# A fused perceiver layer: TensorE's upper-layer loop turned to begin with the token steps, one score run of eight, and the expert-row loads moved to the end of a turn

## The chip, the cores and the metric

The kernel runs on one core of one Trainium2 chip. The metric is the device time of one execution in microseconds (us); lower is better. TensorE is called PE, VectorE DVE, ScalarE ACT, GpSimd POOL and SyncE SP.

## The reference, cut to what matters

All tensors are float32. 32 sequences of 64 tokens with 512 features go through three residual blocks:

```python
x = x + cross_attention(layernorm(x), ctx)     # ctx: 32 x 1601 x 512, one head of 512
x = x + self_attention(layernorm(x))           # 16 heads of 32, causal, with a bias in the denominator
x = x + ffn(layernorm(x))                      # two mixture layers with a gelu between them

def kmoe(x, W, A, B, scale, bias, ...):        # 64 experts, the 2 best of each token
    vals, idx = top_k(x @ W.T, 2); probs = softmax(vals)
    Y = einsum("nkoi,nij,nkpj->nkop", A[idx], xs, B[idx])
    return einsum("nkop,nk->nop", Y, probs).reshape(...) * scale + bias
```

In the upper mixture layer a normalised row pair of tokens (1024 numbers, a 32 x 32 matrix) is multiplied by its expert's A (64 x 32) from one side and by B (64 x 32) from the other; the lower layer goes back from 64 x 64 to 32 x 32.

## The kernel before, in words

The program is written per engine: each engine runs its own list of instructions in order, and semaphores hold the lists together. No planner sets the order; it stands in the code.

**Cross attention** (lines 560 to 789). The 32 sequences are worked on in 16 pairs p. Of each pair the context stands in two halves (7 and 6 tiles of 128 rows), each in one of five slots of SBUF. DVE transposes the context in blocks (`blocks`, L600 to 609, two transposes for a step), PE multiplies a block with the queries (`score`, L590 to 598, 16 steps for a pair), DVE takes the greatest (`greatest`) and later the denominator (`denominator`, after the blocks of step 6), ACT takes exponentials, and PE multiplies the probabilities with the 13 context tiles (`attend`, L755 to 763). PE's list for pair p is: transposes of the probabilities of p - 1, then the 16 score steps of p with the tiles of p - 1 between them, then the last six tiles (L776 to 784). The transposed blocks lie in a ring of four places; for the pairs 2 to 12 (`WIDE`) it has nine. Each tile that PE has finished raises `s_pv`, and SP's transfer of the context three halves ahead waits for that count: a first part (4 tiles) after the fourth tile, a second after the seventh (L653 to 657). The rest rows of a sequence go as five small transfers (L207).

**Self attention** (to about 834 us) is not touched.

**The mixture layers.** The upper layer goes in four turns T of 512 tokens' rows. PE's list for a turn (L2414 to 2448):

1. `gather_up`, eight times: products with one-hot choices that gather B for each token. POOL stages the tables two ahead (`stage_table`, L1880 to 1883), ACT copies the results out (L2165).
2. `rows` (L1535): transposes of the x3 rows of turn T + 1. They read `x3s`, which SP loads (L1829 to 1835) when DVE has transposed it (`s_xt`), PE has transposed it (`s_xf`) and PE has gathered three times (`s_gu`).
3. For T > 0, `logits_dn` (L2261): the lower layer's router logits of turn T - 1, unrolled, 128 products (256 matmuls and 256 weight loads). Then the upper layer's logits of T + 1 (L1551), `fold_dn` (L2269) and `turn_logits` (L1561).
4. `steps_up` (L2383 to 2387): eight laps of an inner loop with two token steps each: `first_up` (L2298), ACT's copy (L2181), `second_up` (L2317), DVE's bias (L2021), ACT's gelu (L2192, L2186). POOL copies the operands of both products (`stage_a`, L1909, and `stage_b`, L1917).
5. Transposes of the one-hot choices of T + 1 and T - 1 (L1568).

Items 2 and the upper half of 3 are skipped by a condition in turn 3, `logits_dn` in turn 0. The rows of the experts' A come by indirect transfers that POOL issues (`experts_rows`, L1391, four a turn, 1 MB each); DVE transposes each into a factor (`factor_a`, L1402), and `stage_a` can start when all four are done. POOL's loads 0 and 1 of turn T + 1 stand in steps 7 and 8 of turn T, load 2 behind the last step, and load 3 in turn T + 1 when two factors are done. SP's list for turn T is: load x3 for T + 1, store the four quarters of the activations h (1 MB each, L1839), and in turn 0 only also store x2 and x3 of the last quad (L851) and wait until they have landed. SP's waits before the x3 load:

```python
                sp.wait_ge(s_xt, 8 * T + 8)
                sp.wait_ge(s_xf, 4 * T + 4)
                sp.wait_ge(s_gu, 8 * T + 3)
```

Of the kernel before, what the change touches and what calls it, by code (L numbers as in the profile page):

```python
# [25 lines left out]
SPARE = {}  # L26
# [532 lines left out]
def cross(nc, block, sem, zone, area, spare, more, temp, ps, a, ident, qbias, halves, slots, qs, s_c, s_qs, s_qd, early):  # L559
# [178 lines left out]
    def _(pe):  # L738
# [33 lines left out]
        for p in range(1, PAIRS):  # L772
# [3 lines left out]
            for g in range(4):  # L776
                transpose_prob(p - 1, g)
            for db in range(STEPS_S):
                if db in (4, 8):
                    for j in ((0, 1, 2, 3) if db == 4 else (4, 5, 6)):  # L780
                        attend(p - 1, j)
                score(pe, p, db)
            for j in range(7, TILES):
# [914 lines left out]
def mixture(nc, block, arena, early, ps, a, first, rest, out):  # L1698
# [105 lines left out]
    def _(sp):  # L1804
# [23 lines left out]

        for T in range(T_N):  # L1829
            if T + 1 < T_N:  # L1830
                sp.wait_ge(s_xt, 8 * T + 8)
                sp.wait_ge(s_xf, 4 * T + 4)
                sp.wait_ge(s_gu, 8 * T + 3)
                for t in range(2):
                    sp.dma_start(x3s[:, t, :], x3_d[2 * T + 2 + t, :, :]).then_inc(s_x3, 16)
            if T + 1 < T_N:
                for q in range(4):
# [33 lines left out]
    def _(pool):  # L1871
# [95 lines left out]
        for T in range(T_N):  # L1967
# [7 lines left out]
            for n in range(STEPS):  # L1975
                stage_b(T, n)
                if n + 2 < STEPS:
                    stage_a(T, n + 2)
                if n == 6 and T + 1 < T_N:
                    exponential("up", T + 1)  # L1980
                if n in (7, 8) and T + 1 < T_N:
                    experts_rows(T + 1, n - 7)
                if n == 10 and T:
                    exponential("dn", T - 1)
            if T + 1 < T_N:
                experts_rows(T + 1, 2)
                stage_table(T + 1, 0)
                stage_table(T + 1, 1)
        for j in range(EARLY):
            stage_unit(j)  # L1990
        stage_unit(EARLY)
# [263 lines left out]
    def _(pe):  # L2255
# [113 lines left out]
        def second_dn(n, u):  # L2369
# [10 lines left out]
                                         start=True, stop=True)  # L2380
            last.then_inc(s_s2, 1)

        def steps_up(T):  # L2383
            with pe.Fori(T * 8, T * 8 + 8) as i:
                first_up(i * 2)
# [25 lines left out]

        pe.wait_ge(early.s_t, 12 * 16)
        pe.wait_ge(s_fold, 2)
        with pe.Fori(0, T_N) as T:  # L2414
            pe.wait_ge(s_ohe["up"][0], T + 1)
            pe.wait_ge(s_bias, T * STEPS + CREDIT)
            apart(pe, SPARE)
            with pe.Fori(T * 2, T * 2 + 2) as j:
                gather_up(j * 4, 0)
                pe.wait_ge(rest.r2, rest.r2_all)  # L2420
                gather_up(j * 4 + 1, 1)
                gather_up(j * 4 + 2, 2)
                for e in range(2):
                    pe.wait_ge(s_ohe["dn"][e], T - 1 + CREDIT)
                gather_up(j * 4 + 3, 3)
            with pe.If(T < T_N - 1):
                for t in range(2):
                    pe.wait_ge(s_geu, T * 8 + 5 + t + CREDIT)
                    rows(pe, T + 1, t, ROW_BANKS[2 * t:2 * t + 2])
            pe.wait_ge(s_geu, T * 8 + 8 + CREDIT)  # L2430
            with pe.If(T > 0):
                pe.wait_ge(s_gelu, T * STEPS)
                pe.wait_ge(s_wr, 32)
                apart(pe, SPARE)
                logits_dn(4)
            with pe.If(T < T_N - 1):
                logits_up_turned(pe, T + 1, 6)
            with pe.If(T > 0):
                fold_dn(T, 7)
            with pe.If(T < T_N - 1):  # L2440
                turn_logits(pe, T + 1, 6)
            steps_up(T)
            with pe.If(T < T_N - 1):
                transpose_choices(pe, "up", 2, T + 2)
            with pe.If(T > 0):
                with pe.If(T < T_N - 1):
                    pe.wait_ge(s_bias, T * STEPS + STEPS + CREDIT)
                    transpose_choices(pe, "dn", 6, T)
        with pe.Fori(0, 2) as p:
            for b in range(4):  # L2450
                unit_first(p, b)
# [54 lines left out]
```

## Time and profile before

| | us |
|---|---|
| three runs | 1232.98, 1235.85, 1237.30 (median 1235.85) |
| the profiled execution | 1234.49 |
| its span in the profile | 1232.7 |
| PE, PE's weight loads | 1165.7, 774.0 busy |
| DVE, ACT, POOL | 790.9, 508.4, 286.0 busy |
| mean granted clock of PE | 0.987 of full |

A row of a timeline has: start in us, duration in us, engine, line, operation, output <- input (partitions x elements), the number of instructions merged, and in brackets how long the engine had been idle before it and what released it ("issue": nothing that the profile shows). Two neighbouring groups of PE overlap a little, since matmuls are pipelined; start to start is the better measure. SPq is SP issuing transfers. Where several issues are merged, the duration covers the waits between them. A row of a table by stretches has: stretch, its length, busy us and instructions of PE, PE's weight loads, DVE, ACT and POOL, the granted clock of PE as a share of full speed (1.00 is the level of 2.4 GHz, 0.50 that of 1.2 GHz), the share of the DMA engines that is busy, and GB/s.

### The profile page before, as it was taken

What the parts mean: (1) busy time and instruction counts of PE and PEld (TensorE: products, weight loads), DVE (VectorE), ACT (ScalarE), POOL (GpSimd) and SP (SyncE); (2) the same over time, 40 slices, a digit from 0 to 9 for tenths busy, and PEclk for the clock granted to TensorE, in tenths of its full rate; (3) what the DMA queues carried; (4) which work ended last, traced back from release to release, by engine and by line L of the source; (5) the groups of instructions that cost most, each with busy time, mean ns of one, the idle gap of its engine ahead of it and who ended that gap; (6) DMA issues with size and microseconds to landing.
All of it is one profiled execution on the core that took longest, in us unless ns stands there. A gap on an engine that the chain in (4) does not pass through costs nothing.

```text
span 1232.7 us, 59579 instructions
## 1 busy us (share of the span) xinstructions
PE 1165.7 (95%) x26847; PEld 774.0 (63%) x26847; DVE 790.9 (64%) x1551; ACT 508.4 (41%) x904; POOL 286.0 (23%) x461
## 2 busy tenths in 40 slices
PE   9999999999999999999999999997888888899995
PEld 6865444434444434666766676675777777789995
DVE  5566777577766774255555555565748686477775
ACT  2323543544344532222212221233647556466763
POOL 1000000000000001022212221223626536246555
PEclk9999999999999999999999999998899999999998
DMA  7886788868887794401110111044627253144423
GB/s 290 277 279 214 254 305 293 291 240 302 298 297 256 268 339 139 105 11 58 68 68 6 62 68 51 35 130 147 237 104 259 109 211 137 48 125 120 120 60 77
DMA packets 65104, 208.33 MB, mean 169 GB/s; under 512 B 11664, under 2 KB 28048, under 8 KB 50864
## 3 DMA queue, kind: packets, MB, share of 16 engines
q1 hardware_dynamic: 62704, 190.24, 45.2%
q0 software_dynamic: 2304, 16.78, 4.0%
q8 instruction: 65, 1.06, 0.3%
q14 instruction: 31, 0.25, 0.1%
HBM read 173.42 MB, written 33.55 MB: 168 GB/s over the span
## 4 chain that ended last, share of the span: by engine, by line
PE 83%; DVE 5%; POOL 3%; issue 3%; DMA 2%; ACT 2%; SPq 1%; DVEq 0%; POOLq 0%; ACTq 0%
PE ps L760 15%; PE ps L596 13%; PE ps L1133 9%; PE ps L2331 5%; PE ps L2365 5%; PE ps L266 5%; PE ps L1247 4%; PE ps L1154 4%; PE ps L508 3%; PE ps L2261 2%; PE ps L2378 2%; PE ps L752 2%; PE ps L2317 2%; DVE arena L2021 2%; PE ps L2298 2%
## 5 line engine op out<-in xcount | busy, mean ns | idle before, releaser
L608 DVE STREAM_TRANSPOSE arena<-arena 128x448 f32<-128x448 f32 (+1 forms) x512 | 257.5, 573 | 27.2 <-PE ps L596 27.1
L760 PE MATMUL ps<-arena 128*64 128x512 f32 x832 | 189.2, 598 | 0.0
L596 PE MATMUL ps<-arena 32*64 32x400 f32 (+1 forms) x4096 | 186.9, 500 | 2.2 <-DVE arena L608 2.0
L596 PEld LDWEIGHTS ps<-arena 32*64 32x64 f32 x4096 | 82.4, 131 | 99.7 <-issue 58.8
L713 ACT COPY arena<-arena 32x2048 f32<-32x2048 f32 x42 | 79.7, 1898 | 138.3 <-DMA arena<-q_n 137.6
L760 PEld LDWEIGHTS ps<-arena 128*64 128x64 f32 x832 | 55.7, 136 | 121.2 <-issue 121.2
L1133 PE MATMUL ps<-arena 128*128 128x256 f32 x512 | 114.2, 381 | 0.8 <-ACT arena L1068 0.8
L934 POOL TENSOR_TENSOR arena<-arena 128x1024 f32<-128x1024 f32 x8 | 19.0, 2369 | 388.1 <-PE ps L760 388.1
L1133 PEld LDWEIGHTS ps<-arena 128*128 128x128 f32 x512 | 96.4, 190 | 17.2 <-issue 3.3
L2181 ACT COPY arena<-ps 128x512 f32<-128x512 f32 x128 | 75.0, 587 | 58.8 <-PE ps L2298 32.4
L2021 DVE SCALAR_TENSOR_TENSOR arena<-ps,arena 128x512 f32<-128x512 f32 x64 | 70.6, 1128 | 36.2 <-PE ps L2317 36.1
L614 DVE TENSOR_REDUCE arena<-ps 128x1 f32<-128x401 f32 (+1 forms) x64 | 32.3, 567 | 82.0 <-PE ps L596 82.0
L2331 PE MATMUL ps<-arena 64*64 64x32 f32 x4096 | 70.3, 218 | 2.7 <-issue 2.7
L2331 PEld LDWEIGHTS ps<-arena 64*64 64x64 f32 x4096 | 68.9, 135 | 3.2 <-issue 2.9
L2031 DVE COPY arena<-ps 128x512 f32<-128x512 f32 x64 | 44.3, 692 | 37.3 <-PE ps L2365 35.2
L1002 DVE SCALAR_TENSOR_TENSOR arena<-ps,arena 128x512 f32<-128x512 f32 x32 | 20.6, 686 | 70.2 <-PE ps L1144 70.2
L631 ACT ACTIVATE arena<-ps,arena 128x384 f32<-128x384 f32 x64 | 36.3, 581 | 70.8 <-DVE arena L622 70.8
L952 POOL TENSOR_TENSOR arena<-arena 128x512 f32<-128x512 f32 x32 | 33.3, 1042 | 138.5 <-DVE arena L1019 138.5
L2365 PE MATMUL ps<-arena 64*64 64x128 f32 x1792 | 61.9, 274 | 0.0
L266 PE MATMUL ps<-arena 128*128 128x512 f32 x128 | 60.2, 605 | 0.0
L1154 PE MATMUL ps<-arena 128*64 128x256 f32 x512 | 58.8, 380 | 0.0
L1247 PE MATMUL ps<-arena 128*128 128x512 f32 x128 | 57.8, 593 | 0.8 <-ACT arena L1109 0.8
(163 smaller groups left out, 1895.7 us busy)
## 6 DMA issues: line engine op xcount, KB each, us to landing
arena<-ctx SPq DMA_DIRECT2D x64, 1024.0 KB
arena<-ctx SPq DMA_DIRECT2D x32, 768.0 KB
h_n<-arena SPq DMA_DIRECT2D x12, 1024.0 KB
arena<-h_n SPq DMA_DIRECT2D x12, 1024.0 KB, 5.1
arena<-x SPq DMA_DIRECT2D x16, 512.0 KB, 4.4
arena<-ctx SPq DMA_DIRECT2D x32, 256.0 KB
x_n<-arena SPq DMA_DIRECT2D x16, 512.0 KB, 3.5
arena<-q_n SPq DMA_DIRECT2D x22, 256.0 KB, 11.0
```

The lines of the kernel that those rows point to most:

```text
L266: x = pe.matmul(ps[:, par, :], early.ats[:, c, par::2], early.xwv[:, c, :], start=c == 0, stop=c == DC - 1)
L596: last = pe.matmul(ps[b * SEQ:(b + 1) * SEQ, tb, 0:WIDTH[tb]], qs[p % 2][r, db, b * SEQ:(b + 1) * SEQ], z[PLACE[at]][r, b, 0:WIDTH[tb]], s ...
L608: vec.transpose(z[PLACE[at]][:, :, g * 224:g * 224 + nt * 32].rearrange("p b (j t) -> p b j t", t=32), slots[slot_of(k)][:, :, 0:nt, db * ...
L713: act.copy(qs[p % 2][tb * 32:(tb + 1) * 32, :, :], qs[p % 2][0:32, :, :]).then_inc(s_copied, 1)
L760: last = pe.matmul(ps[b * SEQ:(b + 1) * SEQ, OB, :], probt[:, j, b * SEQ:(b + 1) * SEQ], slot[:, b, jj, :], start=j == 0, stop=j == TILES - 1)
L1133: last = pe.matmul(ps[:, bank, m % 2 * QROWS:(m % 2 + 1) * QROWS], w[n][:, c, m * P:(m + 1) * P], lnt[:, c, :], start=c == 0, stop=c == DC ...
L1154: last = pe.matmul(ps[e * SEQ:(e + 1) * SEQ, 2 + pair, s2 * 256:(s2 + 1) * 256], lnt[:, c, at:at + SEQ], w["swv"][:, c, :].rearrange("p (m ...
L1247: last = pe.matmul(ps[:, (OUT if more else LAST_OUT) + par, :], aot[:, c, par::2], w["swo"][:, c, :], start=c == 0, stop=c == DC - 1)
L2021: vec.scalar_tensor_tensor(h[:, q, :, at].rearrange("p j g -> p g j"), ps[:, b:b + 2, :].rearrange("p b (g x) -> p (b g) x", x=2 * F1)[:, ...
L2181: act.copy(mid[u].rearrange("p (b x) -> p b x", b=2), ps[:, 2 * u:2 * u + 2, 0:256]).then_inc(s_me, 1)
L2331: last = pe.matmul(ps[k * F1:(k + 1) * F1, 2 * u + t, g * D1:(g + 1) * D1], st_h[u][rows_t, g * F1:(g + 1) * F1], two(st_a[u])[rows_t, k, ...
L2365: last = pe.matmul(ps[q * E:(q + 1) * E, 6 + hf, o * P:(o + 1) * P], slots_dn[slot][r, o, :], oh_st[r, 2 * q:2 * q + 2, :].rearrange("p k ...
```

## The change

Four edits. In cross attention PE's seven tiles of a pair stand in one group between two runs of eight score steps, where they stood as four and three between runs of 4, 4 and 8. SP's x3 load waits for the second gather, and for each half only for the DVE transpose that read that half. POOL's row loads 0, 1 and 2 all stand behind the last step of a turn and behind two table copies. PE's loop over T is turned: gather, rows and logits of turn 0 stand as straight code ahead of it; its body (three laps) begins with the steps and ends with the gather, rows and logits of the next turn; the steps of turn 3 stand behind it. PE executes the same matmuls in the same order.

```diff
@@ -776,8 +776,8 @@
             for g in range(4):
                 transpose_prob(p - 1, g)
             for db in range(STEPS_S):
-                if db in (4, 8):
-                    for j in ((0, 1, 2, 3) if db == 4 else (4, 5, 6)):
+                if db == 8:
+                    for j in range(7):
                         attend(p - 1, j)
                 score(pe, p, db)
             for j in range(7, TILES):
@@ -1828,10 +1828,10 @@
 
         for T in range(T_N):
             if T + 1 < T_N:
-                sp.wait_ge(s_xt, 8 * T + 8)
                 sp.wait_ge(s_xf, 4 * T + 4)
-                sp.wait_ge(s_gu, 8 * T + 3)
+                sp.wait_ge(s_gu, 8 * T + 2)
                 for t in range(2):
+                    sp.wait_ge(s_xt, 8 * T + 4 + 4 * t)
                     sp.dma_start(x3s[:, t, :], x3_d[2 * T + 2 + t, :, :]).then_inc(s_x3, 16)
             if T + 1 < T_N:
                 for q in range(4):
@@ -1978,14 +1978,13 @@
                     stage_a(T, n + 2)
                 if n == 6 and T + 1 < T_N:
                     exponential("up", T + 1)
-                if n in (7, 8) and T + 1 < T_N:
-                    experts_rows(T + 1, n - 7)
                 if n == 10 and T:
                     exponential("dn", T - 1)
             if T + 1 < T_N:
-                experts_rows(T + 1, 2)
                 stage_table(T + 1, 0)
                 stage_table(T + 1, 1)
+                for m in range(3):
+                    experts_rows(T + 1, m)
         for j in range(EARLY):
             stage_unit(j)
         stage_unit(EARLY)
@@ -2380,6 +2379,24 @@
                                          start=True, stop=True)
             last.then_inc(s_s2, 1)
 
+        def gather_tile(T):
+            pe.wait_ge(s_ohe["up"][0], T + 1)
+            pe.wait_ge(s_bias, T * STEPS + CREDIT)
+            apart(pe, SPARE)
+            with pe.Fori(T * 2, T * 2 + 2) as j:
+                gather_up(j * 4, 0)
+                pe.wait_ge(rest.r2, rest.r2_all)
+                gather_up(j * 4 + 1, 1)
+                gather_up(j * 4 + 2, 2)
+                for e in range(2):
+                    pe.wait_ge(s_ohe["dn"][e], T - 1 + CREDIT)
+                gather_up(j * 4 + 3, 3)
+
+        def next_rows(T):
+            for t in range(2):
+                pe.wait_ge(s_geu, T * 8 - 3 + t + CREDIT)
+                rows(pe, T, t, ROW_BANKS[2 * t:2 * t + 2])
+
         def steps_up(T):
             with pe.Fori(T * 8, T * 8 + 8) as i:
                 first_up(i * 2)
@@ -2411,41 +2428,31 @@
 
         pe.wait_ge(early.s_t, 12 * 16)
         pe.wait_ge(s_fold, 2)
-        with pe.Fori(0, T_N) as T:
-            pe.wait_ge(s_ohe["up"][0], T + 1)
-            pe.wait_ge(s_bias, T * STEPS + CREDIT)
+        gather_tile(0)
+        next_rows(1)
+        pe.wait_ge(s_geu, 8 + CREDIT)
+        logits_up_turned(pe, 1, 6)
+        turn_logits(pe, 1, 6)
+        with pe.Fori(0, T_N - 1) as T:
+            steps_up(T)
+            transpose_choices(pe, "up", 2, T + 2)
+            with pe.If(T > 0):
+                pe.wait_ge(s_bias, T * STEPS + STEPS + CREDIT)
+                transpose_choices(pe, "dn", 6, T)
+            gather_tile(T + 1)
+            with pe.If(T < T_N - 2):
+                next_rows(T + 2)
+            pe.wait_ge(s_geu, T * 8 + 16 + CREDIT)
+            pe.wait_ge(s_gelu, T * STEPS + STEPS)
+            pe.wait_ge(s_wr, 32)
             apart(pe, SPARE)
-            with pe.Fori(T * 2, T * 2 + 2) as j:
-                gather_up(j * 4, 0)
-                pe.wait_ge(rest.r2, rest.r2_all)
-                gather_up(j * 4 + 1, 1)
-                gather_up(j * 4 + 2, 2)
-                for e in range(2):
-                    pe.wait_ge(s_ohe["dn"][e], T - 1 + CREDIT)
-                gather_up(j * 4 + 3, 3)
-            with pe.If(T < T_N - 1):
-                for t in range(2):
-                    pe.wait_ge(s_geu, T * 8 + 5 + t + CREDIT)
-                    rows(pe, T + 1, t, ROW_BANKS[2 * t:2 * t + 2])
-            pe.wait_ge(s_geu, T * 8 + 8 + CREDIT)
-            with pe.If(T > 0):
-                pe.wait_ge(s_gelu, T * STEPS)
-                pe.wait_ge(s_wr, 32)
-                apart(pe, SPARE)
-                logits_dn(4)
-            with pe.If(T < T_N - 1):
-                logits_up_turned(pe, T + 1, 6)
-            with pe.If(T > 0):
-                fold_dn(T, 7)
-            with pe.If(T < T_N - 1):
-                turn_logits(pe, T + 1, 6)
-            steps_up(T)
-            with pe.If(T < T_N - 1):
-                transpose_choices(pe, "up", 2, T + 2)
-            with pe.If(T > 0):
-                with pe.If(T < T_N - 1):
-                    pe.wait_ge(s_bias, T * STEPS + STEPS + CREDIT)
-                    transpose_choices(pe, "dn", 6, T)
+            logits_dn(4)
+            with pe.If(T < T_N - 2):
+                logits_up_turned(pe, T + 2, 6)
+            fold_dn(T + 1, 7)
+            with pe.If(T < T_N - 2):
+                turn_logits(pe, T + 2, 6)
+        steps_up(T_N - 1)
         with pe.Fori(0, 2) as p:
             for b in range(4):
                 unit_first(p, b)
```

## Rows read from the trace of the kernel before

**Rows 1.** The page's busy times, all engines.
```profile
PE 1165.7 (95%) x26847; PEld 774.0 (63%) x26847; DVE 790.9 (64%) x1551; ACT 508.4 (41%) x904; POOL 286.0 (23%) x461
```
**Rows 2.** Timeline of PE in one wide pair of cross attention.
```profile
329.93 2.94 PE L596 MATMUL ps<-arena 32*64 32x401 f32 x64
332.80 3.66 PE L760 MATMUL ps<-arena 128*64 128x512 f32 x16
336.39 2.94 PE L596 MATMUL ps<-arena 32*64 32x401 f32 x64
339.26 2.80 PE L760 MATMUL ps<-arena 128*64 128x512 f32 x12
342.00 5.63 PE L596 MATMUL ps<-arena 32*64 32x401 f32 x128
```
**Rows 3.** Timeline of PE in turn 0 of the upper layer, before the steps.
```profile
851.59 0.51 PE L1551 MATMUL ps<-arena 128*64 128x128 f32 x5 [3.91 <-issue]
...
858.77 1.72 PE L2298 MATMUL ps<-arena 32*32 32x64 f32 x128
```
**Rows 4.** Timeline of PE: ends of the steps of turns 1 and 3.
```profile
917.32 1.48 PE L2298 MATMUL ps<-arena 32*32 32x64 f32 x128
...
934.07 0.76 PE L2317 MATMUL ps<-arena 64*64 64x64 f32 x32 [1.55 <-POOL arena L1917]
...
945.18 0.65 PE L1568 MATMUL ps<-arena 128*128 128x128 f32 x4
...
1019.59 1.49 PE L2298 MATMUL ps<-arena 32*32 32x64 f32 x128
...
1044.16 0.69 PE L2317 MATMUL ps<-arena 64*64 64x64 f32 x32 [0.48 <-DVE arena L2021]
```
**Rows 5.** Timelines of SP and PE around the x3 load, turns 1 and 2.
```profile
898.63 0.81 SPq L1835 DMA_DIRECT2D arena<-x_n  x2
...
903.74 3.63 PE L1535 MATMUL ps<-arena 128*128 128x128 f32 x16 [2.94 <-DMA arena<-x_n]
...
957.38 1.96 PE L1535 MATMUL ps<-arena 128*128 128x128 f32 x16 [0.18 <-DMA arena<-x_n]
```
**Rows 6.** Timelines of DVE and PE in pair 13, four places in the ring.
```profile
409.36 0.12 DVE L678 TENSOR_REDUCE arena<-arena 128x1 f32<-128x6 f32 x1
...
417.39 6.09 PE L596 MATMUL ps<-arena 32*64 32x401 f32 x128
```
**Rows 7.** Timelines of DVE and SP in the pair of rows 2.
```profile
325.05 7.01 DVE L608 STREAM_TRANSPOSE arena<-arena 128x448 f32<-128x448 f32 x14
...
345.94 2.04 SPq L207 DMA_DIRECT2D arena<-ctx  x5
...
350.18 7.01 DVE L608 STREAM_TRANSPOSE arena<-arena 128x448 f32<-128x448 f32 x14
```
**Rows 8.** Timeline of POOL: the first factor copies of turns 0 and 3.
```profile
851.75 2.07 POOL L1909 COPY arena<-arena 128x512 f32<-128x512 f32 x2 [7.10 <-DVE arena L1402]
...
1016.96 1.22 POOL L1909 COPY arena<-arena 128x512 f32<-128x512 f32 x2 [6.76 <-DVE arena L1402]
```
**Rows 9.** Table by stretches: clock, DMA share and GB/s in two stretches.
```profile
890.00:893.00 3.00, 2.95 (x117) 2.98 (x125) 3.00 (x3) 0.93 (x1) 0.29 (x1) 0.53 0.99 407
934.00:938.00 4.00, 3.84 (x192) 3.37 (x192) 2.63 (x6) 1.70 (x4) 3.53 (x6) 0.57 1.00 268
```
**Rows 10.** Timeline of PE in the lower layer's first pass.
```profile
1067.75 0.43 PE L2331 MATMUL ps<-arena 64*64 64x32 f32 x16 [1.33 <-issue]
```
**Rows 11.** DMA queues, 934.5 to 938.5 us: packets, MB, share of the engines.
```profile
q0 software_dynamic: 129, 0.96, 94.6%
q1 hardware_dynamic: 2, 0.02, 1.0%
```
**Rows 12.** Instruction queues in 845 to 852 us and, second, in 862 to 1045 us.
```profile
q8 instruction: 2, 0.03, 2.1%
...
q14 instruction: 5, 0.04, 0.1%
```

## The prediction

> **What bounds the kernel now.** Read first the page's busy times: TensorE (PE) is busy 95% of the span [rows 1]; whatever moves the end moves PE's own instructions or the gaps between them. Then read PE's instructions in order of time, for the two places that are edited.
>
> *Cross attention* (to about 490 us). PE never waits. A pair of sequences from p = 2 to 12 ("wide", up to nine blocks ahead) is a fixed string: 4 score steps, 4 context tiles, 4 score steps, 3 tiles, 8 score steps, 6 tiles [rows 2]. Only PE's own pace counts.
>
> *Upper layer* (834 to 1045 us), four turns T. See four kinds of gap. In turn 0, PE stops for 3.91 us before the logits and begins the token steps only at 858.77 [rows 3]. In the steps, VectorE's and POOL's work nearly hides, but in the middle PE waits 1.55 us for POOL's copies [rows 4], because POOL issues two indirect row loads there. Between the steps of turn 0 and of turn 1, PE waits 2.94 us for the x3 rows, which SP could load only after two stores had landed [rows 5]. Between turns 1 and 2 that wait is 0.18 us: on time, with nothing to spare [rows 5].
>
> **The change, part by part.** Against the profiled execution (1234.49 us).
>
> *1. Score runs: one of 8 in place of 4 + 4.* In a wide pair, the stretch from the first score to the third run is 342.00 - 329.93 = 12.07 us. A run of 64 matmuls takes 2.87 (start to start), one of 128 takes 5.56 (its 5.63 less the 0.07 that two groups overlap); 16 context matmuls take 3.59, 12 take 2.74, so 28 take 3.59 + 12 x 0.215 = 6.17. New sum 11.73: 0.34 less, times 11 pairs, 3.7 us gained [rows 2]. VectorE begins a pair's blocks at 325.05, 4.9 us ahead of PE, one step (two transposes) per 1.0 us, so step 8 is there at 333.3 [rows 7] where PE wants it at 334.8: hidden. Pairs 1, 13, 14 and 15 have four places only; there a run of 8 already waits for VectorE and takes 6.09 rather than 5.63. The new first run adds the denominator's two short operations (0.12, and I take the other alike) in VectorE's way: 5.56 + 0.46 + 0.24 + 6.17 = 12.43, 0.36 more, times 4, 1.4 lost [rows 2, 6]. Net **-2.3** (bounds -3.7 and 0). The slot's transfer is released later: its first part after the fourth tile, at 329.93 + 5.56 + 3.59 = 339.1 where it was 336.4, its second after the seventh, at 341.7 where it was 342.0. SP's last issue for it ends at 345.94 + 2.04 = 348.0 now and no later then; the block that reads it starts at 350.18 + 0.5. Hidden, with some 2 us for the last and smallest piece to land [rows 2, 7]; if that cover went, each wide pair would lose what lies beyond.
>
> *2. The loop turned.* The order of PE's instructions stays the same; only what is loop, skip and straight code changes. Before, turn 0 jumped over the unrolled lower-layer logits (512 instructions), and the gap of 3.91 us in which PE waited for nothing visible follows that jump. Now turn 0's part stands straight. PE is free at 847.68 and has about 3 us of logits work; next late is POOL, whose second copy ends at 851.75 + 2.07 = 853.82 [rows 3, 8]. Steps then start at 853.9 rather than 858.77: -4.9. PE will have idled in pieces before, and where it idles the granted clock falls (a stretch at 0.57 lies behind the 1.55 us wait [rows 4, 9]); I charge 0.9 for that. **-4.0** (bounds -5 and 0).
> Price of the turning: the backward jump now lies between one transpose and the steps, where before it lay behind 8 transposes; nothing in the trace shows it bare. Ends: nothing, or a first-pass gap such as the 1.33 us in the lower layer [rows 10] at each of two jumps; I take 0.4, being nearest to the inner loop's jumps, which show nothing. The last turn's steps are a new copy, run for the first time: one such gap, 1.3 (0 to 3.9). **+1.7**.
>
> *3. POOL's row loads 0 and 1 leave steps 7 and 8 for the end of the turn, behind two table copies, with load 2.* The steps of turn 1 take 945.18 - 917.32 = 27.9 us, those of turn 3, which has no such loads, 1044.16 + 0.69 - 1019.59 = 25.3 [rows 4]. Turns 0, 1 and 2 are alike; of the 2.6 some 0.2 is the second pow operation that turn 1 keeps. 3 x 2.4 = **-7.2** (bounds -8.3 and -5.5). Queued behind the moved loads on POOL are only table copies that PE wants once it has gathered from the two that are made ahead: nothing.
>
> *4. What the moved loads collide with.* They now start some 1.5 us before the steps end, three in a row, 3.1 MB, where one (1 MB) was in flight. In that stretch SP also sends the last quarter of h (1 MB) and, after turn 0, x2 and x3 (1 MB), and waits for their landing before it loads the next x3 rows. The trace shows who yields: with two row loads queued the software queue holds 94.6% of the engines for 4 us and the hardware queue 1.0%, while SP is in the midst of its four h stores [rows 11]. Rates: 407 GB/s, and 268 where the two kinds meet [rows 9]; I take 0.36 MB/us. So 2.1 MB more stand ahead: 5.8 us.
> Turn 1: SP gets past the landing of x2 and x3 at 898.63; that comes 5.8 us later, and the load behind it meets a little more traffic: **+6.0** (bounds +3 and +8.5) at PE's wait before 903.74 [rows 5].
> Turn 2: x3 rows land at 957.38 after a load that SP issued only once VectorE had read the old rows; by then the engines had run dry for, as I estimate, 1.6 us, so 5.8 - 1.6 = 4.2. The SP edit (second gather in place of third, each half as soon as its transpose is done) sends half of it 1.1 us earlier, into the same queue: nothing. PE then idles over 4 us and the row transposes take 3.63 as in turn 1 instead of 1.96 [rows 5]: **+5.9** (bounds +1 and +9).
> Turn 3: no x3 load. VectorE's factors come about 1 us later; POOL's two copies, done at 1018.18, have 1.4 us to spare before the steps [rows 4, 8]. **+0.5** (0 to 2).
> Turn 0's x3 load comes one gather earlier; PE did not wait for it: nothing.
>
> By a rule of the Trainium skill, "DMA: Bandwidth & Descriptors", section "Queues, rings and completion order", each DMA engine goes round the queues that have work and changes at packets. The pair of [rows 11] shows one side alone for 4 us, so the trace bears it out at most at whole transfers; by the rule only about one row load would stand ahead, and the time would be that of the second rival.
>
> **Sum.** -2.3 - 4.0 + 1.7 - 7.2 + 6.0 + 5.9 + 0.5 = +0.6 us: 1235.1 against 1234.49. The three runs have a median of 1235.85, 1.4 above; on that scale 1236.5. A measurement of this kernel can tell about 0.3% (3.7 us) from no change.
>
> **The rivals.**
> *A, slower: the turned loop is fetched again on each lap.* Place: the jump from turn 1's and turn 2's logits to the steps. If the target has gone, the gap of [rows 3] comes back, 3.91 us and again about as much with the next block, on two laps: +13, 1249. It decides once the body no longer stays in the engine. For: two instruction packets ran in 845 to 852 us. Against: from 862 to 1045 the queue that brought them (q8) moved none, over three backward jumps [rows 12], and the body is no longer than it was. 0.10.
> The Trainium skill, "Runtime: NRT & Kernel Launch", section "Instruction fetch mechanics", says that a taken branch whose target is outside the two pages at hand forces a fetch before execution goes on. That would price this rival at every lap; the empty queue of [rows 12] speaks against it here.
> *B, faster: the queues alternate.* h, x2 and x3 pass between the row loads; one load, not two, stands ahead, 2.9 us: turn 1 +3.2, turn 2 +1.3 and +1.7 for the slower transposes. Sum -5.0: 1231 on the scale of the median. For: late packets of both queues are mixed in other stretches. Against: [rows 11]. 0.25.
> *C, the turn doesn't do what it says:* the gap before turn 0's steps comes from the first pass itself, not from the skip. Then -4.0 is gone: +4.6, 1240.5. For: 1.33 us gaps in the lower layer's first pass. Against: these are a third of 3.91. 0.12.
> *D, slower: the contention is deeper.* The fourth row load slips ahead of SP's loads too and the queues meet at 268 GB/s: turn 1 +8.5, turn 2 +8.5: +5.7, 1241.5. 0.13.
>
> **How the numbers follow.** My own sum has 0.40. The predicted time is its 1236.5, its own range 1232 to 1241. B reaches down, C and D up; the range 1229 to 1246 leaves out A and the tails of B. Faster by over 0.3% (below 1232.1): most of B and a bit of mine, 0.25. Slower by over 0.3% (above 1239.6): A, D, most of C, a bit of mine, 0.34. Within: 0.41.
>
> **What would show it.** Wide pairs with a period 0.3 us shorter, narrow ones 0.4 longer; turn 0's steps starting where POOL's second factor copy ends; steps of turns 0 to 2 of 25.5 to 26.5 us; PE's waits for x3 of 8 to 9 us in turn 1 and 4 to 5 in turn 2, with SP's landing of x3 late; instruction packets beside turn 3's steps only. Wrong if x3's waits stay below 4 us (B), if the gap stays before turn 0's logits (C), or if q8 is busy in turns 1 and 2 (A).

## The result and the profile after

The changed kernel takes 1238.03 us (median of 20 runs, 1235.81 to 1240.39), the kernel before 1235.69 on the same chip (20 runs). The ratio is 1.0022, interval 1.0012 to 1.0031: 0.22% slower, within the 0.3% that were called no change, and 1.5 us above the predicted 1236.5. The profiled execution took 1238.09 with a span of 1236.3, 3.6 more than before's 1232.7.

A small sum of large terms, then, as forecast. First the page's busy times, which answer to [rows 1]: PE does 3.7 us less in a span that is 3.6 longer, so it waits some 7 us more.

```profile
PE 1162.0 (94%) x26847; PEld 776.4 (63%) x26847; DVE 790.8 (64%) x1551; ACT 508.8 (41%) x904; POOL 283.9 (23%) x461
```

The timeline of PE in a wide pair, as [rows 2], and below it in the narrow pair 13, where [rows 6] stood. The columns are start, us, engine, line, what is computed, count, and in brackets the idle time before with its releaser.

```profile
328.15 5.63 PE L596 MATMUL ps<-arena 32*64 32x401 f32 x128
333.71 6.24 PE L760 MATMUL ps<-arena 128*64 128x512 f32 x28
339.89 5.63 PE L596 MATMUL ps<-arena 32*64 32x401 f32 x128
...
402.52 5.10 PE L596 MATMUL ps<-arena 32*64 32x401 f32 x112
407.93 0.93 PE L596 MATMUL ps<-arena 32*64 32x401 f32 x16 [0.31 <-DVE arena L608]
408.80 6.25 PE L760 MATMUL ps<-arena 128*64 128x512 f32 x28
414.97 6.08 PE L596 MATMUL ps<-arena 32*64 32x401 f32 x128
```

The wide stretch is 339.89 - 328.15 = 11.74 (forecast 11.73), the narrow one 414.97 - 402.52 = 12.45 (forecast 12.43), with a stop for VectorE before the last 16 scores of the run.

The timeline of PE in the upper layer: turn 0 up to its steps (as [rows 3]), the way into turn 1, the way into turn 2, and the start and end of turn 3's steps. Lines behind L1830 carry a number one lower than before (L2297 was L2298).

```profile
846.28 1.97 PE L1551 MATMUL ps<-arena 128*64 128x128 f32 x32 [1.15 <-issue]
...
851.58 1.73 PE L2297 MATMUL ps<-arena 32*32 32x64 f32 x103 [2.58 <-POOL arena L1909]
855.22 0.65 PE L2297 MATMUL ps<-arena 32*32 32x64 f32 x25 [1.91 <-issue]
...
883.26 2.53 PE L2280 MATMUL ps<-arena 64*32 64x128 f32 x144 [1.73 <-ACT arena L1522]
890.46 8.30 PE L2280 MATMUL ps<-arena 64*32 64x128 f32 x368 [4.67 <-issue]
904.77 3.68 PE L1535 MATMUL ps<-arena 128*128 128x128 f32 x16 [6.01 <-DMA arena<-x_n]
...
944.56 0.66 PE L1568 MATMUL ps<-arena 128*128 128x128 f32 x4
960.74 3.67 PE L1535 MATMUL ps<-arena 128*128 128x128 f32 x16 [4.20 <-DMA arena<-x_n]
...
1024.80 2.04 PE L2297 MATMUL ps<-arena 32*32 32x64 f32 x128 [0.36 <-POOL arena L1909]
...
1050.82 2.41 PE L2348 MATMUL ps<-arena 64*64 64x128 f32 x80
```

See three things. The 3.91 us of [rows 3] have become 1.15. A stop of 1.91 us stands inside the first pass of the steps, at their 104th matmul, and one of 4.67 inside the first gather of turn 1, the first execution of that copy. And x3 is late by 6.01 and 4.20 us.

The gap of [rows 3] wasn't alone. A second one stood before the other 27 of the same 32 matmuls (timeline of PE, kernel before), and it is gone as well: 3.91 + 2.59 have become 1.15.

```profile
854.70 3.25 PE L1551 MATMUL ps<-arena 128*64 128x128 f32 x27 [2.59 <-issue]
```

Read as a ledger, with turn by turn the steps and the "front" (from the end of one turn's steps to the start of the next):

| us | before | after | difference |
|---|---|---|---|
| span's start to turn 0's steps | 858.77 | 851.58 | -7.2 (1.8 of it in cross attention) |
| steps of turn 0 | 28.9 | 29.3 | +0.4 |
| front of turn 1 | 29.7 | 38.1 | +8.4 |
| steps of turn 1 | 27.9 | 25.6 | -2.2 |
| front of turn 2 | 24.1 | 31.3 | +7.2 |
| steps of turn 2 | 28.2 | 25.6 | -2.5 |
| front of turn 3 | 22.1 | 23.3 | +1.1 |
| steps of turn 3, and the rest | | | -0.3, -1.4 |

The sum of the differences is +3.6 before rounding. About 1 us of the first row is scatter between traces: run 2 below, which changes nothing ahead of turn 0's steps, starts them at 857.62, 1.15 earlier than the kernel before.

Who is ahead of x3? The timelines of POOL and of SP around the end of turn 0's steps (which is at 880.87). POOL issues three row loads in a row, SP its two stores of x2 and x3, and 14.46 us later, when they have landed, the load.

```profile
879.18 1.08 POOL L1391 DMA_INDIRECT arena<-a_up,arena  x1 [0.16 <-issue]
880.56 0.94 POOL L1391 DMA_INDIRECT arena<-a_up,arena  x1 [0.30 <-issue]
881.80 0.94 POOL L1391 DMA_INDIRECT arena<-a_up,arena  x1 [0.30 <-issue]
...
896.87 0.97 POOL L1391 DMA_INDIRECT arena<-a_up,arena  x1 [0.15 <-issue]
```

```profile
883.46 1.50 SPq L851 DMA_DIRECT2D x_n<-arena  x2
897.92 0.82 SPq L1835 DMA_DIRECT2D arena<-x_n  x2
```

Before, the stores were issued at 890.29 and the load at 898.63 [rows 5], 8.34 later. And the DMA queues (packets, MB, share of the engines), first in 883 to 887 us, where only the software queue moves data though SP's h and x stores are already issued, then in 888 to 892 us, where both do:

```profile
q0 software_dynamic: 163, 1.21, 89.8%
...
q1 hardware_dynamic: 108, 0.88, 52.2%
q0 software_dynamic: 109, 0.76, 47.1%
```

Where nothing stands beside them the same stores start at once: in run 5 they are issued at 856.32, and in 857 to 858 us the hardware queue has 87.2% of the engines.

### The profile page after: what moved, and what is told of

It reads as the page before. It is cut to its first block, busy times and chain, and to the rows that moved or that the text cites. A ratio compares the mean times of both kernels' runs of the same rounds, so it can differ in the third digit from the quotient of the medians.

```text
span 1236.3 us, 59550 instructions
## 1 busy us (share of the span) xinstructions
PE 1162.0 (94%) x26847; PEld 776.4 (63%) x26847; DVE 790.8 (64%) x1551; ACT 508.8 (41%) x904; POOL 283.9 (23%) x461
## 4 chain that ended last, share of the span: by engine, by line
PE 80%; DVE 7%; issue 4%; DMA 3%; POOL 2%; SPq 2%; ACT 1%; DVEq 0%; POOLq 0%; ACTq 0%
PE ps L760 14%; PE ps L596 11%; PE ps L1133 9%; PE ps L2330 5%; PE ps L2364 5%; PE ps L266 5%; PE ps L1247 4%; PE ps L1154 4%; DVE arena L608 3%; PE ps L508 3%; PE ps L2377 2%; PE ps L2316 2%; DVE arena L2020 2%; PE ps L752 2%; PE ps L2260 2%
## 5 line engine op out<-in xcount | busy, mean ns | idle before, releaser
L760 PE MATMUL ps<-arena 128*64 128x512 f32 x832 | 185.8, 596 | 0.0
L266 PE MATMUL ps<-arena 128*128 128x512 f32 x128 | 60.2, 605 | 0.0
```

What stands on the lines that cost most here:

```text
L266: x = pe.matmul(ps[:, par, :], early.ats[:, c, par::2], early.xwv[:, c, :], start=c == 0, stop=c == DC - 1)
L760: last = pe.matmul(ps[b * SEQ:(b + 1) * SEQ, OB, :], probt[:, j, b * SEQ:(b + 1) * SEQ], slot[:, b, jj, :], start=j == 0, stop=j == TILES - 1)
```

## The experiments

Twelve runs in three sets, each set on one chip with runs of the kernel before between them; ratios are to those. "Changed" is the changed kernel.

**1. Score runs alone.** The first hunk of the diff, nothing else:
```
-                if db in (4, 8):
-                    for j in ((0, 1, 2, 3) if db == 4 else (4, 5, 6)):
+                if db == 8:
+                    for j in range(7):
```


> Only the score runs (one of 8 in place of 4 + 4). Theory: wide pairs (2 to 12) 0.34 us shorter each, pairs 1, 13, 14 and 15 0.35 us longer each; in all -1.5 to -2.5 us, and nothing later changes. Rival: the transfer that is released later reaches VectorE's blocks too late and PE waits for them: then the wide pairs save less than 0.2 us each and the whole is 0 to +2 us.

Measured: 1234.37, before 1234.70; ratio 0.9994 (0.998 to 1.0009). Cross attention is 2.0 us shorter (from its first matmul of L752 to the first of L266: 380.28 before, 378.31 here, 378.49 in the changed kernel), and turn 0's steps start 2.1 earlier, at 856.68. Turn 1's start at 917.15, only 0.2 earlier. Timelines of POOL, SP and PE show where the gain went:

```profile
894.79 0.97 POOL L1391 DMA_INDIRECT arena<-a_up,arena  x1 [0.24 <-DVE arena L1402]
...
895.80 0.82 SPq L1835 DMA_DIRECT2D arena<-x_n  x2
...
902.56 3.68 PE L1535 MATMUL ps<-arena 128*128 128x128 f32 x16 [6.11 <-DMA arena<-x_n]
906.16 8.27 PE L2261 MATMUL ps<-arena 64*64 64x128 f32 x256
```

Turn 0's steps end 2.9 us earlier than before (884.76 and 887.64), and the x3 load moves along: 895.80 against 898.63, 2.8 earlier. But here POOL's fourth row load was issued 1.0 us ahead of it, and x3 took 6.76 us to land; before, that load was issued 0.28 behind it, and x3 took 5.11. That is 1.65 of the 2.8. Another 1.0 goes behind the wait, which has grown from 2.94 [rows 5] to 6.11: the 256 matmuls of the lower layer's logits take 8.27 us (granted clock 0.87 in 906.1 to 914.4) where they took 7.27 (1.00 in 907.3 to 914.5). This is one pair of traces; the times alone, with their interval, allow anything from 2.5 us won to 1 us lost.

**2. The row loads alone.** POOL's hunk, on the kernel before; SP's waits stay as they were:
```
-                if n in (7, 8) and T + 1 < T_N:
-                    experts_rows(T + 1, n - 7)
...
-                experts_rows(T + 1, 2)
                 stage_table(T + 1, 0)
                 stage_table(T + 1, 1)
+                for m in range(3):
+                    experts_rows(T + 1, m)
```


> Only POOL's row loads 0 and 1 moved from steps 7 and 8 to the end of the turn. Theory (the moved loads make SP's transfers late): steps of turns 0, 1, 2 shorter by 2 to 3 us each (-7), but PE's wait for the x3 rows rises from 2.94 to about 9 us in turn 1 and from 0.2 to about 5 us in turn 2, row transposes of turn 2 at half clock; in all +4 to +8 us. Rival (x3 is late in the changed kernel because PE's gather of turn 1 ran as first-time code, with a gap of 4.67 us): here that code is resident, the x3 waits stay near 3 and 0 us and the whole is -5 to -7 us.

Measured: 1239.67, ratio 1.0043 (1.0025 to 1.006), +5.3 us by the ratio. Steps of turns 0 to 2: 26.0, 25.6, 25.6, together 7.7 less. Fronts of turns 1 to 3: 37.1, 29.9, 22.9, together 13.9 more; net +6.2 in the trace. The gathers of turn 1 ran without any stop for code, and PE waited all the longer for x3, 11.74 us where about 9 were expected (timeline of PE, turns 1 and 2):

```profile
906.68 3.68 PE L1535 MATMUL ps<-arena 128*128 128x128 f32 x16 [11.74 <-DMA arena<-x_n]
...
962.79 3.45 PE L1535 MATMUL ps<-arena 128*128 128x128 f32 x16 [4.42 <-DMA arena<-x_n]
```

The late x3 is due to the moved loads, and not to the turned loop.

**3. The turn alone.** The two hunks in PE's program only (gather_tile, next_rows and the turned loop).

> Only PE's loop turned. Theory: the gap before the logits of turn 0 goes, steps of turn 0 start right after POOL's second factor copy, 4 to 6 us earlier, run at half clock at first with one gap of about 2 us; the gather of turn 1 has a first-time gap, partly hidden by the wait for x3; 1 us less behind the last step. In all -1 to -4 us. Rival: the first-time code of turn 1's gather and the bare backward jumps (0.5 us each) eat the gain: -1 to +2 us.

Measured: 1228.73, ratio 0.9949 (0.993 to 0.9968), -6.3 us, more than any theory had. (Its profiled execution is the slowest of its seven, and 4.1 us below that of the kernel before.) Timeline of PE before the steps of turn 0 and in turn 1:

```profile
853.45 2.04 PE L2298 MATMUL ps<-arena 32*32 32x64 f32 x128 [2.17 <-POOL arena L1909]
...
892.78 8.13 PE L2281 MATMUL ps<-arena 64*32 64x128 f32 x368 [3.19 <-issue]
901.07 1.96 PE L1535 MATMUL ps<-arena 128*128 128x128 f32 x16 [0.16 <-ACT arena L2165]
```

The steps start 5.3 us earlier. There is no stop inside their first pass here, nor in that of turn 3. The new copy of the gather stops PE for 3.19 us, but in the place of the 2.94 us for which PE waited for x3 before: the front of turn 1 stays 29.7. So the first-pass stop of this copy costs next to nothing. Turn 0's steps end 4.0 us earlier than before (883.67 and 887.64) and turn 1's begin 3.9 earlier (913.38 and 917.32): this gain passes the place of the wait whole. POOL's fourth row load was issued at 899.01 here, 4.0 us behind the x3 load (894.97). And a stop of 1.01 us that stood behind the last step of turn 3 is gone.

**4. Changed, with the row loads back in steps 7 and 8.**

> The changed kernel with POOL's row loads 0 and 1 back in steps 7 and 8. Theory: against the changed kernel the steps of turns 0 to 2 are 2 to 3 us longer each, but PE waits for x3 3 to 4 us in turn 1 and below 1 in turn 2: 6 to 9 us faster than the changed kernel, 3 to 6 us faster than the kernel before. Rival (the moved loads are worth their place): it is slower than the changed kernel.

Measured: 1229.17, ratio 0.9951 (0.9935 to 0.9966), about 9 us below the changed kernel. Fronts 29.6, 24.4 and 22.0, no wait for x3 in turns 1 and 2, where 3 to 4 us and up to 1 were expected. This is the turn with the score runs, and it is as fast as the turn alone: turn 0's steps start 1.9 us earlier than there (851.52) and end at the same time (883.61 and 883.67), since a first-pass stop of 2.11 us stands in them.

**5. Changed, with turn 0's store ahead of the h stores.**
```
+            if T == 0:
+                rest.store_rows(sp)
+                sp.wait_ge(s_out, QUADS * 32)
             (the four h stores)
-            if T == 0:
-                rest.store_rows(sp)
-                sp.wait_ge(s_out, QUADS * 32)
```


> The changed kernel, and turn 0's store of the last activation rows with the wait behind it is moved ahead of the h stores in SP's queue, so that turn 1's x2 and x3 transfers are issued sooner. Theory (x3 is late in turn 1 because its transfer is issued behind the three row loads, which start when turn 0 ends): the 6.0 us wait of the first row matmul of turn 1 shrinks to 0 to 3 us, the 4.2 us wait of turn 2 stays, and the time is 2 to 6 us below the changed kernel's 1238, so 1232 to 1236. Rival (the order in SP's queue is indifferent, since the store itself waits for the row loads on the DMA engines): the wait stays at 5 to 7 us and the time at 1238.

Measured: 1237.56, ratio 0.9981 (0.9971 to 0.9991), by the ratios 5 us below the changed kernel, on another chip. The stores leave at 856.32, before any row load, and x3 is issued 6.2 us behind the end of turn 0's steps (890.20 - 884.04), where the changed kernel needs 17.0; PE no longer waits for it. So much is the order in SP's queue. But the wait of turn 2, which this edit doesn't touch, is gone as well, and so the size of the gain isn't the edit's alone. The timeline of PE at the end of turn 0 shows what else is different:

```profile
878.79 0.60 PE L2316 MATMUL ps<-arena 64*64 64x64 f32 x8
879.77 0.34 PE L2316 MATMUL ps<-arena 64*64 64x64 f32 x5 [0.38 <-issue]
880.48 0.35 PE L2316 MATMUL ps<-arena 64*64 64x64 f32 x6 [0.37 <-issue]
881.21 0.35 PE L2316 MATMUL ps<-arena 64*64 64x64 f32 x6 [0.38 <-issue]
881.94 0.36 PE L2316 MATMUL ps<-arena 64*64 64x64 f32 x5 [0.38 <-issue]
```

PE goes by five or six matmuls and stops for 0.37 us, for nothing that the profile shows, while the row loads run (issued at 878.53, 879.91 and 881.15); the last step's second half takes 5.2 us in place of the changed kernel's 1.5. The same stands in turns 1 and 2. The steps take 30.3, 28.9 and 28.5 us, and the gain of the moved loads is gone; in exchange the loads are issued 5.1 us before the end of turn 1's steps (944.57 - 939.50) and not 1.8 (944.56 - 942.79), so that less of them is left in front of x3.

**6. SP's waits alone.**
```
-                sp.wait_ge(s_xt, 8 * T + 8)
                 sp.wait_ge(s_xf, 4 * T + 4)
-                sp.wait_ge(s_gu, 8 * T + 3)
+                sp.wait_ge(s_gu, 8 * T + 2)
                 for t in range(2):
+                    sp.wait_ge(s_xt, 8 * T + 4 + 4 * t)
```


> The kernel of before, with nothing changed but SP's waits ahead of the x2 transfers (one per half). Theory: nothing, 1234.7 plus or minus 1, and the step spans within 0.3 us. Rival: the earlier start of the first half is worth up to 1 us in each of turns 1 and 2 (1232.5), or it meets the row loads and costs as much.

Measured: 1239.57 against 1239.73, ratio 0.9997 (0.9984 to 1.0011): nothing, as forecast. It served as the trace of before on this chip, and gave one more pair for x3. Timelines of POOL, SP and PE:

```profile
900.42 0.96 POOL L1391 DMA_INDIRECT arena<-a_up,arena  x1 [0.35 <-DVE arena L1402]
...
900.60 0.81 SPq L1835 DMA_DIRECT2D arena<-x_n  x2
...
908.20 3.68 PE L1535 MATMUL ps<-arena 128*128 128x128 f32 x16 [5.31 <-DMA arena<-x_n]
```

POOL's load was 0.18 us ahead, and x3 took 7.60 us.

**7. Changed, with the first of the three loads back in step 7.**
```
+                if n == 7 and T + 1 < T_N:
+                    experts_rows(T + 1, 0)
...
-                for m in range(3):
+                for m in (1, 2):
```


> The changed kernel, with the first of the three row loads issued in step 7 again and the other two left at the end of the turn. Theory (what counts is the bytes that stand in the queue ahead of x3): the x3 wait of turn 1 falls by a third to a half from 6.0 us (3 to 4), that of turn 2 from 4.2 to 1 to 2, the steps of turns 0 to 2 are some 1.2 us longer each (half of what two loads cost); the time is 1234 to 1237. Rival (the queue is held by whatever is in it, one load or three): waits as in the changed kernel, steps longer, 1239 to 1241.

Measured: 1234.57, ratio 0.9969 (0.9953 to 0.9985). There is no wait for x3 in turns 1 and 2 at all; from the x stores to the x3 load it is 883.90 to 893.30, 9.4 us, against 14.5 with three loads and 8.3 with one. "By a third to a half" was wrong: both waits are gone. The two loads were issued 6.5 us ahead of the x stores (883.90 - 877.36), where the three of the changed kernel begin 4.3 ahead (883.46 - 879.18): more of fewer bytes had passed. Part of that lead is the slow last step of this chip (steps 29.9, 28.3, 28.2), so what a load's worth of bytes costs can't be read from this run.

**8. Changed, without moved loads, with the early store, and with runs of eight in wide pairs only.**
```
-                if db == 8:
-                    for j in range(7):
+                if p in WIDE:
+                    if db == 8:
+                        for j in range(7):
+                            attend(p - 1, j)
+                elif db in (4, 8):
+                    for j in ((0, 1, 2, 3) if db == 4 else (4, 5, 6)):
```


> The changed kernel without its moved row loads (they stand in steps 7 and 8 again), with the early store of turn 0, and with the one score run of eight only in the wide pairs 2 to 12, the narrow ones as before. Theory: the turned loop keeps its 5.5 to 6 us, no x3 wait stands in turns 1 and 2, and the narrow pairs no longer give anything back (1.4 us less than with runs of eight everywhere): 1227 to 1229 us. Rival (the score run gives nothing wherever it stands, and the store in front delays turn 0's h): 1229 to 1231.

Measured: 1231.06, ratio 0.9931 (0.9918 to 0.9944) on a chip where before took 1239.73. In microseconds the expectation missed, since it was written for a faster chip; 8.6 us below before is more than it had.

Runs 5 to 8 left a question: the stop and go of run 5 was in every kernel of that set and in none of the first. So the ends of the ladder were run once more, each rung beside its neighbour.

**9 to 12. A ladder on a third chip.** Changed again; with the loads back in steps 7 and 8 (as 4); with the edit of run 8 to the score runs besides; with the early store besides (as 8).

> The changed kernel once more, as the upper end of a ladder of four on one chip. Ratio to the kernel before 1.001 to 1.004. In its trace: the row loads issued 1.5 us after the last step's first matmul, as in the run with the early store. Theory A (the stop-and-go of TensorE in the last step, six matmuls and 0.37 us idle, belongs to kernels in which the loads' transfers meet that step): it is absent here, the steps of turns 0 to 2 are 29, 25.6 and 25.6 us. Theory B (it belongs to the other chip of the second set of runs): the kernel can't tell, and steps of 28 to 29 us may stand here too.

> The changed kernel with its row loads back in steps 7 and 8: the second rung. Ratio to the kernel before 0.994 to 0.997, some 7 to 9 us below the first rung. No x3 wait in turns 1 and 2; steps 28 us, fronts 29.6 and 24.4 us.

> The second rung with the score runs of eight kept only in the wide pairs. Theory (the narrow pairs give back 0.36 us each in four pairs): 0.5 to 1.5 us below the second rung, TensorE's first value matmul (L266) 1.0 to 1.5 us earlier against its first score. Rival: no difference, within 0.5 us.

> The third rung with the early store of turn 0, the same kernel as the earlier run of this combination. Theory (with the row loads in the steps no wait for x3 is left, so the store's place is indifferent): within 1 us of the third rung. Rival (the x3 transfer that lands sooner takes DMA time from the gathers' side): 1 to 2 us either way.

| kernel | median us | ratio to before (1234.23) | interval |
|---|---|---|---|
| 9 changed | 1237.92 | 1.0029 | 1.0015 to 1.0044 |
| 10 row loads back | 1228.10 | 0.9946 | 0.9925 to 0.9967 |
| 11 and runs of eight in wide pairs only | 1227.66 | 0.9946 | 0.9926 to 0.9966 |
| 12 and the early store | 1227.14 | 0.9938 | 0.9918 to 0.9959 |

*9*: the result repeats. The waits for x3 are 6.59 and 4.40, the steps 29.0, 25.6 and 25.6. Its row loads are issued 1.4 to 1.5 us behind the start of the last step's first matmul, as in run 5 (939.50 - 938.04 in turn 1 there), and there is no stop and go. Stops of 0.30 to 0.47 us inside the steps: 13 in run 5, 8 in run 6, 10 in run 7, 8 in run 8, none or one in each of the ten other traces. Run 6 is almost the kernel before, and runs 8 and 12 are the same kernel, with 8 stops there and none here. So theory B holds: they belong to that chip, beside row loads; what they are stays open, and how the changed kernel does there was not run.

*10*: 9.8 us below rung 9. In turn 1 (timeline of PE) the stop for the gather's code stands alone, and x3 is there:

```profile
892.61 7.89 PE L2281 MATMUL ps<-arena 64*32 64x128 f32 x368 [2.91 <-issue]
900.63 1.96 PE L1535 MATMUL ps<-arena 128*128 128x128 f32 x16
```

*11*: cross attention is 1.40 us shorter (377.06 from L752 to L266, against 378.46), the 4 x 0.36 of the prediction; the narrow pair is back to four runs:

```profile
402.08 2.94 PE L596 MATMUL ps<-arena 32*64 32x401 f32 x64
404.95 3.66 PE L760 MATMUL ps<-arena 128*64 128x512 f32 x16
408.55 2.94 PE L596 MATMUL ps<-arena 32*64 32x401 f32 x64
411.42 2.80 PE L760 MATMUL ps<-arena 128*64 128x512 f32 x12
414.15 6.09 PE L596 MATMUL ps<-arena 32*64 32x401 f32 x128
```

But turn 0's steps start only 0.33 us earlier (850.71 and 851.04), and the time doesn't tell the two apart. *12*: within 1 us of rung 11, as expected. PE's program is that of rung 11, but the first-pass stop of 1.91 us that stands in turn 0's steps there is absent here; the steps take 29.4 us for 31.5, and start 0.4 later. Rungs 10 to 12 all beat both kernels; which of the three is best isn't settled.

## Why the prediction was right

The total and its sign against the bound of 0.3% were right; the terms, one by one:

| term | forecast | measured in the changed kernel |
|---|---|---|
| score runs | -2.3 | -1.8 in cross attention |
| turn 0's front | -4.0 | -5.4 at the steps' start (-7.2 less 1.8), +3.3 inside the steps, against run 2 |
| price of turning | +1.7 | 0.4 at each of two jumps; no first-pass stop in turn 3, and 1.0 less behind its steps; the stops are in turns 0 and 1 |
| loads out of the steps | -7.2 | -7.7 in run 2 |
| x3 in turns 1 and 2 | +6.0, +5.9 | fronts +8.4, +7.2; in run 2 +7.4, +5.8 |
| turn 3's front | +0.5 | +1.1 |

**Score runs.** The terms of a pair were right to 0.02 us in wide and narrow pairs, and run 11 shows the four narrow pairs by themselves: 1.40 us. What failed is the step from there to the end: alone they give 0.3 us of 2.0. The prediction had passed every gain ahead of turn 1 on whole: "2.94 <-DMA x_n" [rows 5] as a gap that moves along with the work ahead of it, and the work behind it at its old pace. In run 1 the x3 load did move along, but its transfer became 1.65 us longer behind POOL's fourth row load, and the logits behind the longer wait took 1.0 longer at a lower clock. In the narrow pairs the cover in VectorE's way got thinner: a stop of 0.31 us stands in the middle of the run.

**The turn.** This is the term that was mis-sized: -2.3 with its price, and -6.3 measured alone (4.1 between the two profiled executions). Its parts failed twice. The start of turn 0's steps was right in kind (they begin where POOL's second copy ends, 849.37 + 2.06, and the gap of 3.91 went). The bare backward jump costs 0.4 us each time (0.49 us before the steps of turn 1, 0.47 before those of turn 2, where [rows 4] has next to nothing), 0.8 for both where 0.4 was taken. But the 1.3 us for a first pass in turn 3 never came; the stops sit where PE first runs the gather's second copy and, in some traces, in turn 0's steps. The stop of 3 to 5 us in the gather was not forecast at all, and it is nearly free, because it takes the place of a wait for x3. Of rival C, that the first pass itself was behind the gap, this much is right: 1.15 + 1.91 us of first-pass stops stand in turn 0 where 3.91 + 2.59 stood (the prediction had read the first alone), and the clock is low behind them (the stretch 852 to 860 us at 0.50):

```profile
852.00:860.00 8.00, 6.09 (x322) 5.41 (x307) 3.82 (x6) 2.26 (x5) 4.80 (x8) 0.50 0.01 4
```

The 0.9 us charged for the clock were too few: turn 0's steps take 29.3 rather than 26.0 (run 2, where the loads are out of them too), and only 1.91 of these 3.3 us are the stop. In run 3, which has no stop in them, they take 30.2 where the kernel before took 28.9.

**The row loads.** The mechanism was right as the prediction put it: 5.8 us more ahead of the landing of the x stores, measured 14.46 - 8.34 = 6.1. PE's wait in turn 1 was to be 8 to 9 us; it is 11.74 in run 2, and 6.01 in the changed kernel only because 4.67 us of stop stand ahead of it. On top came what rival D had described: POOL's fourth row load went out ahead of x3's (896.87 and 897.92), and x3 took 6.85 us instead of 5.11. Five traces with it ahead (changed, runs 1, 2, 6 and 9) have 6.76 to 7.60, the one with it just behind has 5.11, and in runs 3, 4 and 10, with it 3.6 to 4.0 us behind, x3 was there when PE came, at most 5.7 to 6.1 us after its issue. No run moved this load alone, so the order is the likely cause and not a shown one. Forecast for the moved loads was +5.2 in all; alone they cost 5.3 by the ratio, on top of the turn 9.8. The difference isn't in x3's transfer. From the end of the steps to the row transposes the moved loads add 7.0 and 4.3 us in turns 1 and 2 of run 2, and 6.6 and 4.1 between run 4 and the changed kernel. It is behind them: from the transposes to the next steps they add 0.4 and 1.5 us in run 2, and 1.9 and 2.9 in the turned kernel. There, in run 4, PE had not waited in turn 1 and the transposes took 1.97 us; in the changed kernel they take 3.68, which the kernel before had paid already (3.63), and turn 2's logits take 8.40 instead of 7.27, at a granted clock of 0.86. Smaller parts are 0.7 us less relief in the steps, 0.6 in turn 3's front and 0.7 in its steps.

So the sum was right by luck, through two errors that met: the turn gives 4 us more, and in its company the loads cost 4 us more.

**The rivals.** A fell: the instruction queue q8 moved 5 packets from 862 to 919 us, where PE first runs the copies of the gather, the transposes and the logits, and 1 from there to 1050. The sign "beside turn 3's steps only" had forgotten that these copies are new too. The page of the Trainium skill that was set against [rows 12], "Runtime: NRT & Kernel Launch", section "Instruction fetch mechanics", would have a fetch at every such jump; in all the turned kernels the stop between the loop's jump and the steps' first matmul stays between 0.47 and 0.57 us, against 1.2 to 4.7 for the stops in code that is run for the first time. B fell in its size, as three loads did hold the stores for over 13 us, but its rule is seen at work from 888 us on, with 52.2% and 47.1%. By the Trainium skill's "DMA: Bandwidth & Descriptors", section "Queues, rings and completion order", the queues take turns at packets all the time; the 89.8% for one of them in 883 to 887, with 2 MB of stores issued on the other, speak against that for the first 4 us. D had the right mechanism; the fronts (+8.4, +7.2) lie at its +8.5 in turn 1 and between forecast and rival in turn 2.

## What to carry to other kernels

A wait in front of an engine isn't a cost that adds up. Ask of everything ahead of it whether the transfer that ends it moves along. A stop of 3 us in the gather, which hardly held x3's transfer, was nearly free. A gain ahead of the transfer's issue is passed on, as the 4 us of run 3 were, unless the transfer meets other traffic by it: in run 1 the load left 2.8 us earlier and the next steps began 0.2 earlier. And where several transfers are moved to a quiet moment, list what the other queues send at that moment and who waits for its landing: 7.7 us of relief inside the steps cost 13.9 us between them. Split a change whose parts meet at one wait, and take the parts that pay: without the moved loads this one is 0.5% faster than the kernel before.

## What was not expected of the hardware

- The first pass of a copy of code stopped PE for 1.3 to 4.7 us in the midst of short matmuls (the 104th of the steps, the 145th of the gather). For the gather it was 4.67 and 3.06 in two traces of the same changed kernel, 2.91 to 4.54 with the row loads back in the steps, and 1.33 in run 7. More DMA traffic beside it doesn't make it longer in any order that these runs show.
- Such a stop can be absent for the same loop: turn 0's steps stopped for 1.9 to 2.5 us in the changed kernel and runs 4, 9, 10 and 11, and not at all in runs 3, 5, 7, 8 and 12. Runs 5, 7 and 9 have the PE program of the changed kernel and run 12 that of run 11, so PE's own code doesn't decide it; what does stays open.
- After three indirect loads (issued from 879.18 to 881.80) the software queue had 89.8% of the engines in 883 to 887 us and the hardware queue nothing; in 888 to 892 they had 47.1% and 52.2%.
- On one of the three chips of the experiments PE stops for 0.3 to 0.5 us between small matmuls while row loads run, 8 to 13 times in each of the four traces there, in run 5 after every five or six matmuls; it was also the slowest, at 1239.73 us for the kernel before where the others took 1234.2 and 1234.7.
